# A message-passing kernel: no scratch fills on GpSimd in two passes, and one more pass with its running sum's mask in PSUM

## The reference, cut to what matters

```
h = relu(layernorm(x)); x = x + L0(h)      # message = h[src] * edge_weight * weight
h = relu(layernorm(x)); x = x + L1(h)      # tensor product with edge_attr_8, sum by source row
h = relu(layernorm(x)); x = x + L2(h)      # relational: msg = (h[src] @ W_rel[type]) * e
h = relu(layernorm(x)); x = x + L3(h)      # kernel network, four steps:
    w = kernel_net(edge_attr_6).reshape(-1, 16, 16)         # once
    for i in range(4):
        msg = einsum('ei,eio->eo', nodes[src], w)
        agg = segment_sum(msg, dst) * inv_deg
        nodes = gelu(agg + nodes @ root_W[i] + root_b[i])
```

## Time and profile before

### The profile page before, as it was taken

The page is one execution under the profiler, slowest core; times in us unless marked ns, Lnnn a source line. Parts: engine busy times, 40 slices in busy tenths (PEclk is TensorE's granted clock), DMA queues, the critical chain, the costliest instruction groups (busy, mean ns, idle before and its releaser), DMA issues. The chain is left out here.

```text
span 24892.2 us, 403534 instructions
## 1 busy us (share of the span) xinstructions
PE 21275.5 (85%) x110422; PEld 11977.0 (48%) x110422; DVE 17478.9 (70%) x29340; ACT 14674.0 (59%) x24676; POOL 19392.5 (78%) x21213
## 2 busy tenths in 40 slices
PE   7999578888888999988888888799979999688886
PEld 4555255555555666654444444344434444333333
DVE  6555378888877888875555555688868888566665
ACT  7888411111115777754444444788868888577775
POOL 6777678888886888877777777777777777788887
PEclk9999789999999999998999998899989999898997
DMA  3222145555552222223333333566656666455554
GB/s 101 42 42 42 39 89 95 92 93 94 92 92 69 75 75 75 75 63 106 114 115 113 114 114 112 161 199 199 199 154 200 201 200 200 137 162 164 162 162 125
DMA packets 2192586, 2964.43 MB, mean 119 GB/s; under 512 B 778166, under 2 KB 1678244, under 8 KB 2190948
## 3 DMA queue, kind: packets, MB, share of 16 engines
q1 hardware_dynamic: 1340898, 2776.49, 34.2%
q0 software_dynamic: 782304, 157.92, 9.6%
q10 hardware_dynamic: 69282, 28.92, 0.4%
HBM read 2289.02 MB, written 672.64 MB: 119 GB/s over the span
## 5 line engine op out<-in xcount | busy, mean ns | idle before, releaser
L777 POOL DMA_INDIRECT got<-table,idx x14040 | 13721.3, 977 | 4390.6 <-issue 3967.9
L797 PE MATMUL in_place<-place_hot,tparts 128*128 128x512 fp8e4 x49950 | 11542.9, 390 | 1657.8 <-ACT place_hot L1002 1654.3
L1002 ACT ACTIVATE place_hot<-place_b,far_lanes 128x512 fp8e4<-128x512 f16 x17550 | 10959.5, 704 | 8.5 <-PE in_place L797 8.5
L797 PEld LDWEIGHTS in_place<-place_hot,tparts 128*128 128x128 bf16 x49950 | 4940.3, 101 | 7537.9 <-issue 2331.3
L1606 POOL DMA_INDIRECT added<-rows,add_idx x2160 | 3602.9, 1668 | 717.4 <-issue 659.0
L1178 DVE TENSOR_TENSOR prod<-w_in,rows_p 128x2048 f32<-128x2048 f32 x810 | 1853.1, 2288 | 1638.1 <-ACT rows_p L990 1609.8
L1649 PE MATMUL acc<-hot,spread 128*128 128x392 bf16 x12960 | 2545.2, 350 | 0.0
L1223 DVE TENSOR_TENSOR prod<-wcopy,got 128x1024 f32<-128x1024 f32 x810 | 983.6, 1231 | 1823.1 <-DMA got<-table,idx 1289.5
L1232 DVE TENSOR_REDUCE msg<-prod 128x64 f32<-128x1024 f32 x1620 | 1967.7, 1215 | 41.4
L1191 DVE TENSOR_REDUCE msg<-prod 128x128 f32<-128x2048 f32 x810 | 1853.0, 2288 | 105.4
L866 PE MATMUL wmat<-k,h 128*128 128x256 f32 x6480 | 1785.9, 400 | 0.0
(11 more groups left out here) (250 smaller groups left out, 21552.6 us busy)
## 6 DMA issues: line engine op xcount, KB each, us to landing
w_in<-kept SPq DMA_DIRECT2D x2430, 512.0 KB
kept<-wcopy SPq DMA_DIRECT2D x810, 512.0 KB, 2.7
got<-table,idx POOLq DMA_INDIRECT x14040
attr<-in_edge_attr SPq DMA_DIRECT2D x270, 768.0 KB
place_b<-place_row SPq DMA_DIRECT2D x1350, 128.0 KB
range_b<-range_row SPq DMA_DIRECT2D x1350, 128.0 KB
rows<-in_src_row SPq DMA_DIRECT2D x270, 512.0 KB
sums<-outb SPq DMA_DIRECT2D x1350, 96.0 KB
```

The lines of the kernel that those rows point to most:

```text
L777: pool.indirect_dma_start(out=got[:, r, j * W:(j + 1) * W], out_offset=None, in_=table, in_offset=bass.IndirectOffsetOnAxis(ap=idx[:, r, j ...
L797: mm = pe.matmul(in_place[b][:, h, :], tparts[:, s, t, :], place_hot[:, b, t, h * XC:(h + 1) * XC], start=(t == 0 and s == 0), stop=(t == ...
L1002: ins = act.activation(place_hot[:, b, t, :], place_b[:, b, :], ACT.Abs_reciprocal_sqrt, bias=SB["far_lanes"][:, t:t + 1], scale=HOT_SLOPE ...
```

## The change

No pass fills any more, and every kernel_kept pass (steps 1, 2 and 3 of the last layer) has the mask in PSUM. The relational pass keeps its mask in SBUF. The scratch tile, the memsets, the semaphore `rested` and the waits for it are gone.

```diff
-        edge_pass(nc, a, SB, "weighted", table16, fill=False)
+        edge_pass(nc, a, SB, "weighted", table16)
...
-            edge_pass(nc, a, SB, "kernel_kept" if depth else "kernel_net", table16, fill=depth == 3, psum_mask=depth >= 2)
+            edge_pass(nc, a, SB, "kernel_kept" if depth else "kernel_net", table16)
...
-def edge_pass(nc, a, SB, kind, table, fill=True, psum_mask=False):
+def edge_pass(nc, a, SB, kind, table):
...
-        if fill:
-            rest = sb("rest", [P, J0 * RW])
...
-        if psum_mask:
+        if kind == "kernel_kept":
             mask = [ps(f"mask{k}", [P, 512])[:, 0:F * CW].rearrange("p (f j) -> p f j", f=F) for k in range(HALVES)]
...
-                    if fill and at != 0:
-                        pool.wait_ge(S["rested"], k)
                     pool.sem_inc(S["turn_open"], 1)
                     for j in range(J0):
                         pool.indirect_dma_start(
                             out=got[:, r, j * W:(j + 1) * W], out_offset=None, in_=table,
                             in_offset=bass.IndirectOffsetOnAxis(ap=idx[:, r, j:j + 1], axis=0)).then_inc(got_in[r], 16)
-                        if fill:
-                            ins = pool.memset(rest[:, j * RW:(j + 1) * RW], 0.0)
-                    if fill:
-                        ins.then_inc(S["rested"], 1)
```

More of the change, by code:

```diff
@@ L41 @@
 RING = 4
-RW = 256
 T = -(-E // (P * C * HALVES)) * C * HALVES
@@ L650, in edge_pass @@
                  "attr_used0", "attr_used1", "w_made", "w_used", "h1_made", "h1_ready", "h2_made", "h2_ready",
-                 "hot_made", "hot_used", "out_made", "stored0", "stored1", "dve_step", "run_cleared", "rested", "turn_open", "fetch_open",
+                 "hot_made", "hot_used", "out_made", "stored0", "stored1", "dve_step", "run_cleared", "turn_open", "fetch_open",
                  "place_in0", "place_in1", "range_in0", "range_in1", "places_hot", "in_place_made", "picked_made", "in_row_made", "fetched",
```

## The result

The change takes off 633.6 us where 639 were forecast; the median lies 8 us above the forecast. The page's costliest group answers to the earlier trace rows.

A forecast was written before the change was run, and what follows sets the result against it. POOL was taken to bound steps 1 to 3, PE the relational pass. Savings of 607.0 + 9.9 + 22 = 639 us from the 24924 us median gave 24285 us, range 24250 to 24335 us.

The forecast's parts named there:

- Step 3: Last layer's step 3: without fills on POOL, its limit, the pass becomes as short as step 2, 607.0 us less.
- Step 1: Last layer's step 1: mask in PSUM shortens POOL's gathers, scan time unchanged; 9.9 us less, bounds 5 and 15.
- The relational pass: Relational pass, PE-limited: without fills POOL idles at the carry copy, so PE's stalls go; 22 us less.
- rival 1: Relational pass: gathers still meet the carry copy, so its gain is missing; total 24307 us, chance 0.20.
- Step 0: Last layer's step 0: no term in the forecast; the range allowed some 20 us of difference between executions overall.
- The clock: PE's granted clock: 0.96 expected in step 3, from 0.90 before; a relational clock below 1.00 would show Rival 4.
- rival 2: Relational pass: POOL, not PE, is the limit, so the pass falls 250 us; total 24057 us, chance 0.04.
- rival 3: Step 3: fills only fill POOL's time; gathers' landing or matrix loads set the pace; total 24892 us, chance 0.02.
- Rival 4: Relational pass: PE stalls and its clock falls; 24667 us at 0.90, 25144 us at 0.80; chance 0.04.

The follow-up runs named there:

- Fill alone: The kernel before with only step 3's fills taken out, relational fills and step 1's SBUF mask staying: 24254.32 us against 24869.06, ratio 0.9755.
- width by width: The changed kernel with fills of 64, 128 and 512 columns put back in steps 1, 2 and 3 respectively: 25941.01 us.
- fewer gathers: The changed kernel leaving out one of each chunk's 8 gathers in step 2 and two in step 3: 23685.58 us.

## Why the prediction was right

**Step 3** (forecast −607.0, measured −612.9). Right in mechanism and size. Reading the effect off the sister pass in the same trace was the step that carried the forecast; of the 5.9 us beyond it, 4.5 are the difference between executions that step 2 shows too. Fill alone, width by width, and fewer gathers each confirm POOL's sum as the path. The rival that the fills only filled time is excluded.

**Step 1** (−9.9, measured −16.4). Right in mechanism: the scan's time is the same from PSUM, as said, and POOL's is not. The size was short, and outside the bounds of 5 to 15 that were given for it, by the cut-off gather (1.3 us) and by step 2's 4.5. Within one execution the mask is worth 11.2 us in the kernel before and 14.2 in the run with step 3's fills alone, which is what the gathers that start beside the scan lose there (11.1 and 15.7 us). The Trainium skill's figure by which the scan would be slower from PSUM ("VectorE: DVE Perf Modes", "The TRN2 errata") did not show here either: the scan's median is 590 ns in all three steps after.

**The relational pass** (−22, measured −10.8). PE is the limit, and the chain from a held carry copy to a late scan, late one-hot rows and a stall of PE is right. The failed step is "waits for L1249 (after the carry copy), issues its eight gathers in the next 10 to 11 us and is idle when the next carry copy comes". POOL does not wait for L1249 but for the indices, which DVE makes after the scan and the pick, some 2 us later, and its last gathers still reach the carry. Read copy by copy, 230 of the 270 carry copies start inside a gather after the change, against 202 before.

What went is a hold that came with the fills, and the earlier trace rows was misread as a gather's doing. Its copy starts 0.24 us into a gather. Of the copies that start 0.2 to 0.5 us into one, all 124 of the kernel before took 0.213 to 0.456 us, and all 127 after the change 0.194 to 0.197, as this one:

```profile
9521.77 0.94 POOL L772 DMA_INDIRECT got<-table,idx  x1 [0.30 <-issue]
9522.02 0.20 DVE L1119 COPY msg<-run 128x32 f32<-128x32 f32 x1
```

The run with the relational fills kept has the hold (103 copies, all 0.214 or more), and its length grows with the width of the fill, as shown above. Which part of POOL's work holds the copy there the records do not show. A gather alone holds only a copy that starts later into it, at 0.5 to 0.75 us: over 0.25 us in 17 of 21 copies before and in 36 of 37 after, where just 1 of the other 106 outside both places takes as long. One such chunk after the change:

```profile
9431.87 0.94 POOL L772 DMA_INDIRECT got<-table,idx  x1 [0.30 <-issue]
9432.41 0.43 DVE L1119 COPY msg<-run 128x32 f32<-128x32 f32 x1
...
9434.91 1.02 DVE L1127 TENSOR_TENSOR_SCAN run<-mask,msg 128x416 f32<-128x416 f32 x1
9436.50 0.16 DVE L1096 COPY idx<-src_at 128x12 int32 x1
9437.44 0.94 POOL L772 DMA_INDIRECT got<-table,idx  x1 [3.38 <-DVE idx L1096]
```

```profile
9440.91 4.35 ACT L993 ACTIVATE place_hot<-place_b,far_lanes 128x512 fp8e4<-128x512 f16 x7
9442.27 2.97 PE L788 MATMUL in_place<-place_hot,tparts 128*128 128x512 fp8e4 x13
9445.39 1.48 PE L863 MATMUL wmat<-wrel,onehot 90*128 90x256 bf16 x12
```

ACT's one-hot rows end at 9440.91 + 4.35 = 9445.26. PE's 13 matmuls would be through at 9442.27 + 2.81 = 9445.08 (compare; the trace's pitch is 0.216 us a matmul, not the 0.213 of the prediction, whose sum used 2.81 all the same) and the next group starts at 9445.39, the stall of 0.31 again. With the indices early the pass lost a further 9 us (3482 to 3473.5) and came to 12.750, against the 12.74 that I took as PE's own time. So rival 1 was half true: the gathers meet the carry copy no less than before, and what the pass gained came from the end of the fills' hold, which neither the forecast nor the rival had. That the term still has the forecast's sign is luck in that respect.

**Step 0** (nothing, measured +25.9). No edit touches it, and the second profile of the same kernel has 4268.1 us, below the kernel before's 4289.0. Across the nine profiles in which its code is unchanged it is 4268 to 4315 us, and the gathers' mean in 3000 us of it goes with it (1007 ns at 4268.1, 1018 at 4289.0, 1023 at 4314.9). That the product with two SBUF inputs causes the stretches is shown by the run that took it away. The two profiles of the changed kernel account for the difference: 585 gathers start beside the product in the longer one (1385 ns in the mean, 258 us above 944 in all) and 544 in the shorter (1336 ns, 213 us), which is 45 of the 47 us between them. Why one execution meets more of them than another stays open. The forecast's "some 20 us of difference between executions" was about right, by luck rather than by a row.

**The sum.** Step 0 was the largest error of any term. Against the forecast, steps 1 and 3 gave 12 us more, the relational pass 11 less, step 0 took 26, and the rest, taken as nothing, gave 13; together 11 us less than 639. That the total comes so near is in part luck.

**The clock** went as step 2 had shown: step 3 from 0.90 to 0.96, the relational pass at 1.00. Rivals 2, 3 and 4 found nothing. Rival 4 reckons with 3437 us of PE-bound work, for which no row is given; 269 distances of 12.74 us are 3427, which changes its times by 1 us at 0.90 and 3 us at 0.80.

## What to carry to other kernels

Where one kernel runs the same pass several times with different settings, the sister pass in the same trace is the best price list: it gave 607 of 613 us. An engine's filler instructions are free only where that engine has slack in that pass: the same 2160 fills of 0.328 us, 708 us in all, were worth 613 us in step 3 and 11 to 16 in the relational pass, where they cost by holding up a short copy of another engine. Where GpSimd's gathers set the pace, look for VectorE instructions with two SBUF inputs running beside them, and give them a PSUM input where a copy is there anyway; for a wait of several semaphores, ask which is released last before you place what follows it.

## What the runs showed that was not expected

- A product of two SBUF tiles on VectorE stretches a gather from 0.94 to as much as 2.0 us; read from PSUM, the same product leaves gathers at a mean of 950 ns. That was worth 200 us in step 0, a third of the whole change. The Trainium skill ("SBUF — State Buffer", "Who interferes with whom") says that a VectorE instruction with two SBUF inputs contends with a GpSimd instruction that reads SBUF. The gathers take their indices from the SBUF tile `idx`, and the traces agree: beside the product they last 1345 ns in the mean with two SBUF inputs, and 944 with one.
- The cost of a gather differs between executions by 0.3% (median 944 or 947 ns, both found on one chip), and where POOL is the limit the pass goes with it: with the mask in PSUM and no fills, steps 1 to 3 take 2713 to 2716 us at 944 and 2719 to 2720 at 947.
- A fill on GpSimd held up DVE's short copies for up to 0.12, 0.18, 0.28 and 0.56 us at 64, 128, 256 and 512 columns, at a place in the record where a gather alone holds nothing.
- A memset on GpSimd cost 168, 221, 328 and 541 ns for 64, 128, 256 and 512 columns: 0.83 ns a column and 115 ns fixed.
